# A four-layer graph attention kernel: the stages between the heads written out and skewed, biases and normalizations moved to other engines, and a clip two tiles wide in layer 0

## The reference: what is computed

```python
# L0: 4 heads, keys in chunks of 128
scores = clip(q @ k.T / sqrt(32), -10, 10); scores = where(mask == 0, -10, scores)
attn = softmax(scores, within each chunk); ctx = sum over chunks of attn @ v
out = layernorm(ctx @ Wo.T + bo + x) * gamma + beta
# L1: 4 heads, masked softmax over all 1024 keys, out = attn @ v @ wo.T + bo
# L2: 1 head,  e = leaky_relu(s_i + s_j), s = (h @ W) @ a, masked softmax, elu(att @ Wh)
# L3: 4 heads of the same kind, elu
```

## Time and profile before

| | us |
|---|---|
| median of 3 runs | 3339.29 (3332.55 to 3339.44) |
| the profiled execution, its own time | 3331.45 |
| its span | 3329.7 |
| PE busy | 2419.7 (73%) |
| DVE busy | 2343.6 (70%) |
| POOL busy | 1825.3 (55%) |
| ACT busy | 1523.4 (46%) |
| mean granted TensorE clock | 0.824 |

### The profile page before, as it was taken

The page is one execution under the profiler, slowest core; times in us unless marked ns, Lnnn a source line. Parts: engine busy times, 40 slices in busy tenths (PEclk is TensorE's granted clock), DMA queues, the critical chain, the costliest instruction groups (busy, mean ns, idle before and its releaser), DMA issues.

```text
span 3329.7 us, 92771 instructions
## 1 busy us (share of the span) xinstructions
PE 2419.7 (73%) x33108; PEld 1668.0 (50%) x33108; DVE 2343.6 (70%) x5297; ACT 1523.4 (46%) x2211; POOL 1825.3 (55%) x1733
## 2 busy tenths in 40 slices
PE   4488888786343888888887665888555999998970
PEld 2266666564232554545454443666333666666650
DVE  3299888997665777777776545443675988888866
ACT  2355555553121443434443333444243777777760
POOL 2288777785222565555555333444232877777761
PEclk8688778887766899999998776998666988888985
DMA  6733222221454121211212542110332111111125
GB/s 218 252 92 79 72 70 70 70 69 33 127 162 153 40 56 46 52 49 50 55 46 70 144 129 75 53 46 14 124 112 64 47 47 46 43 40 47 46 44 126
DMA packets 299634, 264.33 MB, mean 79 GB/s; under 512 B 193048, under 2 KB 256792, under 8 KB 299216
## 3 DMA queue, kind: packets, MB, share of 16 engines
q1 hardware_dynamic: 294608, 241.68, 26.4%
q0 software_dynamic: 4608, 16.78, 1.4%
HBM read 162.71 MB, written 95.36 MB: 78 GB/s over the span
## 4 chain that ended last, share of the span: by engine, by line
PE 30%; issue 17%; DVE 12%; ACT 3%; POOL 3%; DMA 1%; DVEq 1%; SPq 1%; POOLq 0%; ACTq 0%
PE ps L1030 10%; PE ps L989 4%; DVE full L1328 3%; DVE full L1318 3%; PE ps L927 2%; PE ps L982 2%; POOL xg L317 2%; PE ps L987 2%; PE ps L941 2%; PE ps L889 1%; PE ps L911 1%; DVE xn L1413 1%; DVE rden L1410 1%; PE ps L973 1%; PE ps L974 1%
## 5 line engine op out<-in xcount | busy, mean ns | idle before, releaser
L317 POOL TENSOR_TENSOR xg<-xc 128x512 f16<-128x512 f32 x1536 | 1580.7, 1053 | 836.1 <-ACT xc L800 703.1
L1030 PE MATMUL ps<-vs,xc 128*128 128x33 bf16 (+1 forms) x13824 | 850.4, 189 | 143.0 <-DVE work L1376 89.7
L1030 PEld LDWEIGHTS ps<-vs,xc 128*128 128x128 bf16 x13824 | 679.2, 101 | 471.2 <-issue 295.2
L1030 PE MATMUL ps<-vs,xg 128*128 128x33 bf16 (+1 forms) x9216 | 778.5, 187 | 0.0
L1030 PEld LDWEIGHTS ps<-vs,xg 128*128 128x128 f16 x9216 | 596.7, 99 | 3.1 <-issue 3.1
L800 ACT ACTIVATE xc<-ps 128x512 f32<-128x512 f32 x512 | 305.7, 597 | 436.7 <-PE ps L974 436.5
L800 ACT ACTIVATE xc<-cv,lift 128x512 f32<-128x512 f32 x512 | 351.2, 718 | 295.1 <-DVE cv L1351 293.8
L1328 DVE CUSTOM_DVE_ANT_0 full<-ps,mask_n 128x512 bf16<-128x512 f32 x512 | 353.0, 690 | 169.2 <-PE ps L941 61.6
L1318 DVE CUSTOM_DVE_ANT_0 full<-ps,mask_n 128x1024 bf16<-128x1024 f32 x320 | 390.4, 1220 | 105.4 <-PE ps L927 76.0
L989 PE MATMUL ps<-qs,sel 128*128 128x512 f32 x640 | 415.5, 651 | 0.0
L1351 DVE SCALAR_TENSOR_TENSOR cv<-ps,mask_t 128x512 f32<-128x512 f32 x512 | 336.3, 684 | 60.4 <-PE ps L970 37.9
(11 more groups left out here) (138 smaller groups left out, 3739.7 us busy)
## 6 DMA issues: line engine op xcount, KB each, us to landing
qs<-q_d SPq DMA_DIRECT2D x224, 128.0 KB
ks<-k_d SPq DMA_DIRECT2D x224, 128.0 KB
part<-row_d SPq DMA_DIRECT2D x40, 512.0 KB
v_d<-vbuf SPq DMA_DIRECT2D x24, 792.0 KB, 4.2
vs<-v_d SPq DMA_DIRECT2D x96, 198.0 KB
q_d<-part SPq DMA_DIRECT2D x32, 512.0 KB
k_d<-part SPq DMA_DIRECT2D x32, 512.0 KB
ctx_d<-xn SPq DMA_DIRECT2D x96, 128.0 KB, 1.7
```

Of the source, the lines that this page charges most:

```text
L317: eng.tensor_tensor(plo[:, r, :], prob[:, r, :], phi[:, r, :], ALU.subtract).then_inc(low_done(layer, u, s)[0], 1)
L1030: mm = pe.matmul(acc, half[:, r, it * P:(it + 1) * P], vs[:, n, at:at + width], start=opens and h == 0 and v == 0, stop=h == 1 and v == 1, ...
```

## The change

1. **Layer 0's clip two tiles wide.** `settle_two` and `exp_two` take two neighbouring banks in one DVE and one ACT instruction. `DEEP` goes from 8 to 16 (also for layers 1 to 3), `LAGS[0]` from 6 to 10, the accumulator banks from two to four (banks 4 to 7), `arg` to eight tiles. `prob` moves to the memory of `part`, its low parts to `xc`, `si8` to `ks`.
2. **Node stages written out**, no loops on the device, and skewed: in step i an engine does parts of graph i + `SKEW` (2 in stage 1, 1 in stages 2 to 4, 0 in stage 0) and of graph i, interleaved as shown below.
3. **Biases of v and of the contraction by PE**: one bf16 matmul of 65 rows for each bank (`with_bias`); a setup splits each bias in three bf16 rows.
4. **Norms by ACT**: eight activations 128 wide with a scale and a bias from columns. POOL makes both columns (`power`: two small operations, the power, a product). Beta is added to x by POOL (`plus_beta`) in stage 1. The elu's exp and relu are both by ACT (`below_zero`).
5. **V split straight from PSUM**, two buffers: ACT rounds, DVE subtracts from PSUM, ACT rounds, POOL subtracts.
6. **Vectors a taken through W once**, at the start (two matmuls, `s_wa`). Stages 2 and 3 lose L889 and L735: rows and columns come from x directly.

```diff
-DEEP = 8
-LAGS = (6, 6, 6, 6)
+DEEP = 16
+LAGS = (10, 6, 6, 6)
+SKEW = (0, 2, 1, 1, 1)
...
+            for k, name in enumerate(("L2_gnn_WT", "L3_gnn_WT")):
+                sp.dma_start(wT[:, k, :], t[name]).then_inc(s_const, 16)
...
+                    if f + 2 < GRAPHS:
+                        used(f)
+                        load_graph(stage, f + 2)
+                    if stage < 4 and i >= 0:
+                        store_parts(i)
...  POOL
+                pool.wait_ge(s_ev["var" + name], ev("var" + name, stage, b))
+                pool.tensor_scalar(r, mv[:, k, :, 1], EPS, None, ALU.add)
+                pool.tensor_scalar(m, mv[:, k, :, 0], -1.0, None, ALU.mult).then_inc(s_powers, 1)
+                pool.tensor_tensor(r, r, expo[:, :], ALU.pow).then_inc(s_powers, 1)
+                pool.wait_ge(s_powers, powers[0])
+                pool.tensor_tensor(m, m, r, ALU.mult
...
+                    if stage == 1 and f < GRAPHS:
+                        plus_beta(f)
+                        power(stage, "0", f)
+                    if stage > 1 and f < GRAPHS:
+                        power(stage, "", f)
+                    if stage < 4 and i >= 0:
+                        last_part(i)
+                    if stage == 1 and 0 <= i + 1 < GRAPHS:
+                        power(stage, "", i + 1)
...  ACT
+                def norm(dst, src, k, name, b):
+                    for it in range(BLOCKS):
+                        ins = act.activation(dst[:, it, :], src[:, it, :], ACT.Identity,
+                                             scale=rstd[:, k, 0, it:it + 1], bias=rstd[:, k, 1, it:it + 1])
+                def below_zero(b):
+                    act.activation(neg[:, :, :], cs[:, b % 2, :, :], ACT.Exp).then_inc(s_ev["ex"], 1)
+                    act.activation(neg[:, :, :], neg[:, :, :], ACT.Relu, scale=-1.0, bias=unit[:, 0:1]
...
+                for i in range(-SKEW[stage], GRAPHS):
+                    f = i + SKEW[stage]
+                    if stage in (1, 2) and f < GRAPHS:
+                        context(f)
+                    if stage > 2 and f < GRAPHS:
+                        below_zero(f)
+                    if stage < 4 and i >= 0:
+                        turned(i)
+                        high_parts(i)
+                        first_part(i)
+                    if stage == 1 and f < GRAPHS:
+                        inner_norm(f)
+                    if stage < 4 and i >= 0:
+                        second_part(i)
+                    if stage == 1 and 0 <= i + 1 < GRAPHS:
+                        outer_norm(i + 1)
+                    if stage > 1 and f < GRAPHS:
+                        outer_norm(f)
...
+                    def exp_two(s):
+                        act.wait_ge(s_av, T - DEEP + 2)
+                        act.activation(prob[:, r:r + 2, :], arg[:, a:a + 2, :], ACT.Exp,
+                                       scale=2.0 * CLIP, bias=lift[:, 0:1]).then_inc(s_exp, 2)
...  PE
+                def with_bias(bank, k):
+                    pe.matmul(ps[:, bank, :].rearrange("p (t f) -> p t f", f=F), ones_b[0:65, :],
+                              bias3[0:65, k, :].unsqueeze(1).to_broadcast([65, IB, F]), start=True, stop=False,
...
+                    if has_f:
+                        turn_context(f, i)
+                    if has_a:
+                        turn_x(i)
+                    if has_f:
+                        contract(f)
+                    if has_a:
+                        (queries_keys if stage < 2 else rows_of)(i)
+                        values_read(i)
+                        by_blocks(0, xT, wts[:, 4 * stage + 2 if stage < 2 else 6 + stage, :],
+                                  2 * stage if stage < 2 else None, "v_ps")
+                        if stage > 1:
+                            columns_of(i)
...
-                                pe.wait_ge(s_chfree, CREDIT + u * (TILES // 2 * UNROLL) + s // 2 - 1)
+                                pe.wait_ge(s_chfree, CREDIT + u * (TILES // 2 * UNROLL) + s // 2 - 3)
...
-                                acc = ps[:, 6 + s // 2 % 2, (s % 2 * IB + it) * 33:(s % 2 * IB + it + 1) * 33]
+                                acc = ps[:, 4 + s // 2 % 4, (s % 2 * IB + it) * 33:(s % 2 * IB + it + 1) * 33]
...  DVE
+            for k in range(3):
+                dve.tensor_copy(cut, given).then_inc(s_fill, 1)
+                dve.wait_ge(s_fill, 13 + 3 * k)
+                dve.tensor_copy(bias3[32 * k:32 * k + 1, :, :], cut[32 * k:32 * k + 1, :, :]).then_inc(s_fill, 1)
+                dve.tensor_tensor(left, given, cut, ALU.subtract).then_inc(s_fill, 1)
...
+                for i in range(-SKEW[stage], GRAPHS):
+                    f = i + SKEW[stage]
+                    if stage and f < GRAPHS:
+                        add_x(f)
+                        statistics(f, 0 if stage == 1 else 1, "0" if stage == 1 else "")
+                    if stage < 4 and i >= 0:
+                        project(i)
+                    if stage == 1 and 0 <= i + 1 < GRAPHS:
+                        scaled(i + 1)
+                        statistics(i + 1, 1, "")
...
+                    def settle_two(s):
+                        dve.wait_ge(s_score, T - CREDIT + 2)
+                        dve.wait_ge(s_exp, T - 2 * RING + 2)
+                        dve.scalar_tensor_tensor(arg[:, a:a + 2, :], ps[:, r:r + 2, :], -0.5,
+                                                 mask_t[:, j:j + 2, c * HALF:(c + 1) * HALF], ALU.max, ALU.min
```

More of the change, by code:

```diff
@@ L729, in project @@
-                        split_v(b)
+                            act.activation(part[:, q, w, 0, :], qk_bank(stage, w), ACT.Identity,
+                                           bias=bcol[:, 2 * stage + w:2 * stage + w + 1]).then_inc(s_ev[name], 1)
                         return
                     n = 2 * HEADS[stage]
-                    act.wait_ge(s_ev["w_ps"], ev("w_ps", stage, b))
-                    act.wait_ge(s_ev["row_ps"], before("row_ps", stage, b))
-                    act.activation(full[:, 0, :], pf[:, 6 * HALF:8 * HALF], ACT.Copy).then_inc(s_ev["w"], 1)
+                    r = pf[0:n, 6 * HALF:8 * HALF]
@@ new lines, in with_bias, with by_blocks @@
+                def with_bias(bank, k):
+                    pe.matmul(ps[:, bank, :].rearrange("p (t f) -> p t f", f=F), ones_b[0:65, :],
+                              bias3[0:65, k, :].unsqueeze(1).to_broadcast([65, IB, F]), start=True, stop=False,
+                              skip_group_check=True)
+                def by_blocks(bank, lhs, w, bias, name):
+                    for it in range(BLOCKS):
+                        if bias is not None and it % IB == 0:
+                            with_bias(bank + it // IB, bias)
+                        mm = pe.matmul(ps[:, bank + it // IB, it % IB * P:(it % IB + 1) * P],
+                                       lhs[:, it * P:(it + 1) * P], w, start=bias is None, stop=True,
+                                       skip_group_check=True)
+                    mm.then_inc(s_ev[name], 1)
@@ L915, in node, with columns_of @@
-                graphs(pe, finish, project)
+                def columns_of(b):
+                    n = 2 * HEADS[stage]
+                    for it in range(BLOCKS):
+                        mm = pe.matmul(ps[:, 4, it * n:(it + 1) * n], xT[:, it * P:(it + 1) * P],
+                                       aa[:, stage - 2, 0:n], start=True, stop=True)
+                    mm.then_inc(s_ev["col_ps"], 1)
+                for i in range(-SKEW[stage], GRAPHS):
+                    f = i + SKEW[stage]
+                    has_f, has_a = stage in (1, 2) and f < GRAPHS, stage < 4 and i >= 0
+                    if has_f:
[9 more added lines that the diff above has]
+                                  2 * stage if stage < 2 else None, "v_ps")
+                        if stage > 1:
+                            columns_of(i)
@@ L1182, in layer_norm, with add_x @@
-                    return ins
-                def finish(b, q, h):
-                    if stage == 0:
-                        return
-                    begin(s_chain_a, CHAIN_A, b)
-                    w, x = work[:, :, :], xr[:, q, :, :]
-                    if stage in (1, 2):
-                        dve.wait_ge(s_load[q], load_at(stage, h))
+                        ins = dve.bn_aggr(mv[:, k, it, :], bns[:, it, :])
+                    done("var" + name, b, ins)
+                def add_x(b):
+                    w, x = wsum[:, b % 2, :, :], xr[:, b % 2, :, :]
+                    dve.wait_ge(s_load[b % 2], load_at(stage, b // 2))
+                    dve.wait_ge(s_ev["xn"], before("xn", stage, b) - 1)
+                    if stage < 3:
@@ L1209, in finish @@
[L1209 to L1215 removed]
+                        done("y", b, dve.tensor_tensor(w, y, x, ALU.add))
+                        return
+                    dve.wait_ge(s_ev["e"], ev("e", stage, b))
```

(20 more changed lines are left out.)

587 lines of the change are left out of this document (268 added, 319 removed).

## The result

3216.5 us, the median of four runs (3215.1 to 3225.6), against 3339.4 (four runs, 3332.6 to 3350.7) for the kernel before: a ratio of 0.9635, 95% interval 0.9603 to 0.9667. The forecast was 3250, 3195 to 3305. The profiled execution has a span of 3223.8 us, 105.9 less than before's 3329.7. The medians differ by more, by 122.8: the profiled execution is the slowest of the changed kernel's four, 9.0 us above their median, and before's lies 7.9 under its own.

What follows compares the result with a forecast made beforehand. DVE and POOL were nearly full in heads(0); chains through several engines set the node stages' pace. Heads(0) -32, node(4) +14, node(1) 0, node(2) -30, node(3) -32, node(0) -8 gave -88: forecast 3250 us, range 3195 to 3305.

Steps and rivals of the forecast that it cites:

- node(1): Node stage 1: one loop through everything of project, 28.7 us a graph against 30.3; change 0, bounds -25 and +40.
- node(0): Node stage 0: two v buffers end ACT's waits for the store, 14.5 us a graph, longer setup; -8 (-17, +6).
- node(4): Node stage 4: ACT's order makes one chain, 13.0 us a graph; eight graphs +14 (bounds +6, +20).
- node(2) and node(3): Node stages 2 and 3: loops of 18.0 and 15.8 us a graph; -30 (-45, -4) and -32 (-44, -20).
- The rival of PE at 1.2 GHz all through the stage: Node stages: PE at its low clock, node(1)'s loop 34 us and +40; total about 3335; chance 0.10.
- The norm on ACT: Norms: 128-wide activations 0.37 us apart, eight for 3.0 us, against DVE's 2.14; bounds 2.1 and 3.7.
- The rule that the prediction had against this move: Norms on ACT: the Trainium skill sends adds and multiplications to VectorE; by its page a norm takes 3.2 us.
- heads(0): Attention stage of layer 0: 604 us from 636, a saving of 32; bounds 15 and 50.
- The pairs: heads(0): two tiles in one DVE operation save 0.05 to 0.06 us a pair; 256 pairs, 15 us.
- The forecast of 8.96 us for eight tiles: heads(0): DVE's own sum for eight tiles, 9.20 less 4 x 0.06 us for the pairs.
- heads(1) and heads(3): Attention stages of later layers: to stay unchanged, since deeper `prob` frees nothing there; 0.
- The rival that heads(0) starves: heads(0): if a pair's way exceeds three pairs, engines take turns; +200, so 3450 us; chance 0.04.

Runs made afterwards that it cites:

- x_n4dve: Against the changed kernel: in node(4) alone VectorE (DVE) makes the norm, in place of ACT; 3192.1 us, ratio 0.9577.
- x_n4ord: Against the changed kernel: in node(4) ACT makes below_zero of the next graph ahead of this graph's norm; 3183.6 us, ratio 0.9534.
- x_n23: Against the changed kernel: in node(2) and node(3) ACT's norm precedes v's second part; in node(3) below_zero stands behind turned; 3224.4 us, ratio 0.9641.
- x_n1: Against the changed kernel: in node(1) the next graph's scaling, statistics and power come ahead of add_x and project, ACT's norm behind turned; 3154.2 us, ratio 0.9449.
- x_n0: Against the changed kernel: in node(0) v's first part waits for the store of the graph before, as with one buffer; 3241.6 us, ratio 0.9704.
- x_blk: Against the changed kernel: layout of the block sums as before (division writes with a stride, sum reads contiguously); 3204.8 us, ratio 0.9596.
- x_lag6: Against the changed kernel: layer 0's lag is six in place of ten, pairs kept; 3228.6 us, ratio 0.9673.
- x_banks2: Against the changed kernel: two accumulator banks in place of four, pairs and lag kept; 3527.4 us, ratio 1.0567.

## Why the prediction came out as it did

The node stages from node(1) on, forecast by writing out their loops, were right in mechanism and nearly in size. The median came out 33.5 us under the forecast: the stages give 18 of that, nearly all of it node(0), and the rest is which execution was profiled, before and after.

- **node(4)**, +14 forecast, +14.8 measured; period 13.0 as forecast. Both ways of breaking the chain (x_n4dve, x_n4ord) took the loss back and more.
- **node(2) and node(3)**, -30 and -32 forecast, -28.7 and -31.2 measured. The periods were 17.1 and 16.0 for 18.0 and 15.8; that PE's turn, v and the norm are the links is read from the program, and x_n23 bears it out for node(2) alone.
- **node(1)**, 0 forecast, +5.5 measured; period 28.3 for 28.7. Part of the agreement is luck: the scaling took 869.28 + 2.97 - 868.03 = 4.2 us for 2.46, where POOL worked beside it, and PE's products up to v took some 2 less than reckoned. That a stage which sheds a quarter of DVE's work gains nothing was the least obvious claim, and x_n1 shows its reason: with the dependency cut the period is 19.0. The rival of PE at 1.2 GHz all through the stage had a loop of 34 us, and that did not come; the clock was 0.65, as before.
- **The norm on ACT**: 0.37 us apart forecast, (3.18 - 0.478) / 7 = 0.386 measured. From the figures of "ScalarE: Activation LUTs" of the Trainium skill, section What ACT_TABLE_LOAD costs, the estimate is 0.186 + 0.107 + 2 x 0.093 - 0.093 = 0.386, and the trace agrees to 1 ns. The rule that the prediction had against this move holds for node(4) as long as ACT's order stays (93.3 us with the norm on DVE, 116.7 on ACT), but ACT in the better order took 78.3. The power chain took 3126.01 - 3123.42 = 2.6 for 2.4.
- **node(0)**, the mis-sized term: -8 forecast, -25.5 measured. The mechanism was named (two v buffers end the waits for the store; x_n0 confirms it), and the loop was put at 12.1 to 13.3. Its own terms add up to 11.75 to 12.95, so the sum was wrong by 0.35, and its lower end is what was measured. Then I raised the period to 14.5, because 11 us a graph of transfers "would need 0.83" of the DMA engines. They gave 1.04, and the period was 11.7: -34 for the seven steps where the forecast had -14. The setup cost 7.2 for 5.5. Nothing in the trace of before said that 0.67 was near a limit.
- **heads(0)**, -32 forecast, -28.4 measured, and here the sum was right by luck. The pairs were to save 15 and bring 9 with the old layout and 1 to 5 with the new; the banks, lag and rings bring 34 where I had 17; the layout, which I read past in the diff, costs 12 to 15. The forecast of 8.96 us for eight tiles failed at 9.13 for the last reason: with the old layout it is 8.95 (x_blk). That the four banks end PE's wait for the division was right (89.7 to 2.0 us), but the same wait came back at the settle (3.2 to 93.4), which the prediction did not have.
- **heads(1) and heads(3)** were to stay and lost 7 and 6 us. heads(3) lies between 687.6 and 694.6 in the changed kernel and its variants, so its 6 are hardly more than that spread. For heads(1) the waits called issue differ, at five places behind the returns of the device loop; in the kernel before, in the changed one, and with single tiles in layer 0:

```profile
PE ps L973 <- issue: 17.3, 5, 3.8
```

```profile
DVE full L1393 <- issue: 15.3, 5, 3.3
```

```profile
DVE full L1393 <- issue: 24.7, 5, 5.1
```

The last two kernels have the same instructions in heads(1) (731.4 and 737.2 us; 735.7 in the other kernel with single tiles, 730 to 733 in the rest), so the difference comes from something outside the stage. It goes with single tiles in layer 0 in every kernel: these waits of DVE are 24.7 and 24.8 us in the two with single tiles and about 15 in those with pairs. So pairs also bring some 5 us in a stage that they don't touch. By what way stays open.

The rival that heads(0) starves named the wrong resource: it put the point at which the engines take turns at the lag, where x_lag6 found 3 to 7 us, and not at the banks, where x_banks2 found 305 with pairs. The pairs and the banks are one edit that only the diff shows as two.

## What to carry to other kernels

Where no engine is full, write out the loop of dependencies with each engine's program order in it; its length forecast four stages here to within 6 us (node(1) in part by luck), and moving the operation that closes the loop was worth more than making one in it faster (one call in node(4) gave 33 us by the medians, four calls in node(1) 62; the faster norm on DVE gave 24). When two tiles are joined into one operation, look at what is ordered behind it on the same engine and who waits for that; the buffers have to grow with it. And price every changed layout in a diff, also where the view's name stays, by the distance between starts in the timeline: durations of overlapping instructions, added up, gave the wrong sign here (+8 us, where the engine's busy time fell by 8).
